# Third layer's loop on ScalarE: the output-weight product moved behind the squares, two convolution taps cut into halves and spread over four tiles

## The reference, cut to what matters

```python
proj = x @ W_in.T + b_in
gate, hBC, dt = proj[..., :INTER], proj[..., INTER:INTER+CONV_DIM], proj[..., INTER+CONV_DIM:]
hBC = silu(sum(xp[:, i:i+S, :] * conv_w[:, i] for i in range(K)))       # xp: hBC padded by K-1 in time
h, Bm, Cm = ...                                                         # split of hBC
...                                                                     # chunked recurrence over time -> y
g = y * silu(gate)
g = g * rsqrt(mean(g * g) + EPS) * norm_w
return g @ W_out.T + b_out
```

## Time and profile before

| | |
|---|---|
| median of 3 runs | 1243.27 us (1240.24 to 1246.04) |
| the profiled execution, its own time | 1239.47 us |
| its span, first to last instruction | 1237.7 us |
| mean granted clock of PE | 0.974 of full speed |
| busy | PE 90%, DVE 72%, ACT 65%, POOL 46% of the span |
| the loop of the third layer | from about 616 to 1060 us of the span, convolutions of tiles 3 to 31 start at 670.00 to 1044.48 |

### The profile page before, as it was taken

The page is one execution under the profiler, slowest core; times in us unless marked ns, Lnnn a source line. Parts: engine busy times, 40 slices in busy tenths (PEclk is TensorE's granted clock), DMA queues, the critical chain, the costliest instruction groups (busy, mean ns, idle before and its releaser), DMA issues.

```text
span 1237.7 us, 14557 instructions
## 1 busy us (share of the span) xinstructions
PE 1116.7 (90%) x4908; PEld 603.6 (49%) x4908; DVE 896.4 (72%) x1364; ACT 804.3 (65%) x1185; POOL 564.5 (46%) x310
## 2 busy tenths in 40 slices
PE   6778899999988999999788999999999999995887
PEld 1323344444334444444465666666666666432554
DVE  3657999999985444424677999899999999324454
ACT  4557667676644443323777999999999999436432
POOL 6002799898951955532014445545545545400000
PEclk8879899999999999999999999999999999998999
DMA  3000655555551211110021112112111111000000
GB/s 127 1 1 15 204 186 178 189 184 192 177 197 45 74 37 43 43 47 1 9 55 55 53 46 60 53 45 60 51 47 60 49 49 48 6 1 1 1 1 34
DMA packets 36664, 84.22 MB, mean 68 GB/s; under 512 B 7109, under 2 KB 13030, under 8 KB 36326
## 3 DMA queue, kind: packets, MB, share of 16 engines
q1 hardware_dynamic: 36590, 83.29, 21.1%
HBM read 80.72 MB, written 2.56 MB: 67 GB/s over the span
## 4 chain that ended last, share of the span: by engine, by line
PE 42%; DVE 28%; ACT 12%; POOL 8%; issue 8%; DMA 1%; SPq 0%; DVEq 0%; POOLq 0%; ACTq 0%
POOL work L729 6%; DVE work L1629 5%; PE ps L1002 4%; PE ps L1018 3%; PE ps L1010 3%; PE ps L1256 3%; DVE work L1701 3%; DVE work L1713 2%; DVE yd L1724 2%; DVE work L668 2%; DVE work L1727 2%; DVE work L1679 2%; PE ps L449 2%; PE ps L1965 2%; ACT work L1462 2%
## 5 line engine op out<-in xcount | busy, mean ns | idle before, releaser
L1800 POOL TENSOR_TENSOR ssum<-ssum,rs 128x1024 f32<-128x1024 f32 x32 | 75.9, 2371 | 205.1 <-DVE work L1629 202.8
L668 DVE TENSOR_TENSOR_SCAN work<-ps,work 128x1024 f32<-128x1024 f32 x64 | 146.6, 2290 | 8.3
L1629 DVE SCALAR_TENSOR_TENSOR work<-work,w_t 128x1024 f32<-128x1024 f32 x96 | 123.3, 1284 | 21.9 <-ACT work L1462 19.3
L449 PE MATMUL ps<-work,ident 128*128 128x512 f32 x256 | 121.7, 598 | 5.6 <-POOL work L729 5.6
L992 POOL TENSOR_TENSOR work<-work,ssum 128x1024 f32<-128x1024 f32 x32 | 76.3, 2389 | 105.6 <-DVE work L1081 57.9
L565 ACT ACTIVATE ps<-work,A 128x1024 f32<-128x1024 f32 x64 | 71.6, 1118 | 72.1 <-DVE work L668 72.1
L1081 DVE TENSOR_TENSOR work<-work,ps 128x512 f32<-128x512 f32 x64 | 43.8, 687 | 99.8 <-PE ps L1010 99.8
L1060 ACT ACTIVATE work<-ps 128x512 f32<-128x512 f32 x64 | 38.1, 597 | 115.4 <-PE ps L1002 115.3
L729 POOL TENSOR_TENSOR work<-work 128x1024 f32<-128x1024 f32 x42 | 99.1, 2362 | 13.6 <-DVE work L668 12.6
L1808 POOL TENSOR_TENSOR yd<-yd,work 128x896 f32<-128x896 f32 x32 | 67.0, 2092 | 45.9 <-DVE work L1727 45.9
L1713 DVE SCALAR_TENSOR_TENSOR work<-ps,work 128x512 f32<-128x512 f32 x128 | 81.9, 681 | 0.0
(11 more groups left out here) (358 smaller groups left out, 2541.5 us busy)
## 6 DMA issues: line engine op xcount, KB each, us to landing
work<-bc_rows SPq DMA_DIRECT2D x42, 512.0 KB, 3.6
work<-sdo_rows SPq DMA_DIRECT2D x64, 224.0 KB, 3.6
yd<-bc_rows SPq DMA_DIRECT2D x22, 512.0 KB, 3.6
rs<-w_rows SPq DMA_DIRECT2D x32, 256.0 KB, 4.1
ssum<-share_rows SPq DMA_DIRECT2D x32, 256.0 KB, 3.1
w_t<-in_tile_w SPq DMA_DIRECT2D x32, 195.5 KB, 2.6
work<-in_w SPq DMA_DIRECT2D x1, 2048.0 KB, 7.6
shared<-in_f SPq DMA_DIRECT2D x3, 512.0 KB, 6.1
```

The source lines that it names most:

```text
L449: mm = pe.matmul(ps[:, YACC + h, :], ident[:, :], HS[u % 4][:, h * BL:(h + 1) * BL], start=(n == 0), stop=(n == DS - 1))
L668: dve.tensor_tensor_scan(h, flat_pair(DABANK), h, 0.0, ALU.mult, ALU.add).then_inc(m0["scan"], 1)
L1629: c = dve.scalar_tensor_tensor(HC[u], HP[:, tap:tap + SEQ], par(u, "taps", tap), HC[u], ALU.mult, ALU.add)
L1800: pool.tensor_tensor(ssum[:, b, :], ssum[:, b, :], rs[:, :, :].rearrange("p k t -> p (k t)"), ALU.add).then_inc(m2["ss"], 1)
```

## The change

In ACT's step, `weights_out` moves from the end of step n, where it made the weights of tile n+1, to the middle of the step, behind `squares(n-1)`, where it makes those of tile n. The call ahead of the loop goes. `bc_first_tap` for the second sequence is cut into four calls of 512 positions, issued between `silu_gate` and `silu_h` in steps 1, 2, 4 and 5; before, two calls of 1024 positions stood at the ends of steps 2 and 3. DVE's wait for the taps follows.

```diff
+        B1_TAP = {1: (0, 0), 2: (0, 1), 4: (1, 0), 5: (1, 1)}
...
-            def bc_first_tap(b, m):
+            def bc_first_tap(b, m, half=None):
                 act.wait_ge(m2["bc_pad"], 4 * (b + 1))
-                source = pad[:, m, K3:K3 + SEQ] if b == 0 else src1[m]
-                act.activation(BCH[m][:, b * SEQ:(b + 1) * SEQ], source, ACT.Copy, scale=V("bc_conv", m * DC + K3)).then_inc(m2["bc_tap"], 1)
+                if half is None:
+                    to, source = BCH[m][:, 0:SEQ], pad[:, m, K3:K3 + SEQ]
+                else:
+                    to, source = blk(BCH[m], 2 * b + half), blk(src1[m], half)
+                act.activation(to, source, ACT.Copy, scale=V("bc_conv", m * DC + K3)).then_inc(m2["bc_tap"], 1)
...
                 if n >= 1:
                     squares(n - 1, 1 - u)
+                weights_out(n, u)
                 if more:
                     silu_gate(n + 1, 1 - u)
+                    if n in B1_TAP:
+                        bc_first_tap(1, *B1_TAP[n])
                     if n in B1_SILU:
                         bc_silu(1, *B1_SILU[n])
                     silu_h(n + 1, 1 - u)
...
-                    weights_out(n + 1, 1 - u)
-                if n in (B1_CONV - 1, B1_CONV):
-                    bc_first_tap(1, n - B1_CONV + 1)
...
             exponentials(0)
-            weights_out(0, 0)
...
-                    dve.wait_ge(m2["bc_tap"], 3 + m)
+                    dve.wait_ge(m2["bc_tap"], 4 + 2 * m)
```

## The result

The changed kernel has a median of 1234.22 us over 8 runs (1232.28 to 1239.06), beside 1244.17 us over 8 runs of the kernel before. The ratio is 0.9933, with a 95% interval of 0.9906 to 0.9959: 8.3 us less on 1243.27, with an interval of 5.1 to 11.7. Forecast were 1237.0 us and a gain of 6.3.

The account below looks back on a forecast made before the run. The circle convolution, transposes, shares, exponentials, `pad_h` was taken to set the pace in plain periods, with ACT delaying 19 of 32 convolutions. Gains 3.0 + 1.5 + 1.8 = 6.3 us off 1243.27 gave 1237.0 us, range 1232 to 1241.

Parts of the forecast that it names:

- part 3: `weights_out` leaves the path ahead of `pad_h` in 16 further steps; gain 1.8 us, bounds 0 and 4.8.
- Part 1: Steps 1 to 2: ACT's 3.3 us wait in `weights_out(2)` for `sum_out(0)` goes; gain 3.0 us, bounds 2.5 and 3.65.
- Part 2: Steps 2 and 3: first taps no longer delay `pad_h`, halves cost nothing; gain 1.5 us, bounds 1.4 and 2.4.
- Part 4: SP's next weights load goes out about 4 us later but lands 4.8 us early; cost 0.
- Rival A: PE sets the circle in plain periods, so the total gain is 4.0 us, 1239.3 us; chance 0.23.
- Rival B: All of `weights_out` comes back as `pad_h` starts sooner behind its product; gain 9.9 us, 1233.4 us; chance 0.17.
- Rival C: Weights land too late and PE waits in some 28 steps; slower, about 1265 us; chance 0.03.
- Rival D: The half taps on ACT are not covered and cost 4.0 us; gain 2.3 us, 1241.0 us; chance 0.12.

Follow-up runs that it names:

- e9: The changed kernel, unchanged, run again; median 1235.37 us of 12 runs, ratio 0.9939 to the kernel before.
- e3: The kernel before with only `weights_out(2)`, the call that waited 3.3 us, moved to the new place; 1238.26 us in one run.
- e2: The changed kernel with `weights_out` back at the end of the step, so only the taps are cut and moved; median 1240.53 us, ratio 0.9986.
- e1: The kernel before with `weights_out` moved, the first taps still whole at the ends of steps 2 and 3; median 1231.18 us, ratio 0.9927.
- e7: The changed kernel with the two first taps whole, between `silu_gate` and `silu_h` in steps 2 and 5; 1238.69 us in one run.
- e4: The changed kernel with `weights_out` making only one column of 128 from tile 2 on; 1234.8 us in one run.
- e5: The changed kernel with `weights_out` of tile n at the end of step n, so the next weights load starts later; 1403.0 us.
- e0: The kernel before, unchanged, run again for its trace; 1246.62 us.
- e8: The changed kernel with DVE's first convolution tap cut into halves for the 16 tiles that waited for ACT; median 1233.2 us, ratio 0.9916.

## Why the prediction was right, point by point

The measured median of 1234.22 us lies in the stated range of 1232 to 1241, but 1.3 us below the 1235.5 to 1238.5 that the forecast had for itself. Faster by over 0.5%, as it came out, had been given 0.43, and within 0.5% 0.52. The mechanism held; the sum was too low in one term (part 3), and the medians of whole executions add a difference of about 1 us that the loop does not explain.

Like with like, that is before and e9, both with the half clock on the shares of step 1, the loop gained 46.70 - 42.37 = 4.33 from tile 2 to 5 and 346.28 - 343.54 = 2.74 from 5 to 31: 7.1 us, with 6.3 forecast.

- **Part 1, the large wait: 3.0 forecast, 3.0 measured** in e3, where only this call is moved. The step by which PE takes back part of the 3.65 at the convolution is there too: 3.45 gained at tile 3, 0.44 given back at tile 4. After has it as well: its tile 4 takes 14.15, where the next one takes 13.43.
- **Part 2, the taps: 1.5 forecast, 1.3 measured** alone (e2), 0.6 on top of the product (e1 against e9), since the moved product by itself already takes 46.70 - 42.97 - 3.0 = 0.7 from the same two steps. Part 1 and 2 together were forecast at 4.5 and came to 4.3. The halves cost nothing that shows at their place, as said; that they had to be halves was not needed (e7).
- **Part 3, the sixteen steps: 1.8 forecast, 2.74 measured.** This is the mis-sized term. For tiles 10, 16, 17, 24 and 31 the step was right, 0.16 to 0.18 each, and tile 18 gave the forecast 0.29. Too low were three counts. Tiles 11 and 12 gained 0.18 and 0.23, where I had 0 for a `silu_h` that ends 0.1 late. It is late (in the plain period of after it starts at 769.26, straight behind the half Silu, with DVE done with the convolution before 769.05), and PE's transposes and DVE's second weighing with it, but `shares` needs only the first weighing and stands 6.86 behind the convolution as before; in e4 a product shorter by 0.11 changes nothing there. Tiles 27 to 29 gained 0.14, 0.23 and 0.16 with 0.08 each forecast, tile 30 0.19 with 0.04, tile 14 0.15 with 0. I had held `project_h` to a fixed distance behind `shares`, and only the bias copy was to move. Steps 25 and 26, PE of before, then PE and ACT of after:

```profile
984.95 1.80 PE L1256 MATMUL ps<-work 128*128 128x128 f32 x14
...
987.60 1.02 PE L1224 MATMUL ps<-work,w_t 128*128 128x512 f32 x2
```

```profile
983.80 1.80 PE L1257 MATMUL ps<-work 128*128 128x128 f32 x14
...
986.39 2.19 PE L1225 MATMUL ps<-work,w_t 128*128 128x512 f32 x4
...
987.46 0.69 ACT L1461 ACTIVATE work<-ps,w_t 128x512 f32<-128x512 f32 x1
```

  The bias stands 1.07 behind the projection, as predicted. But the projection is 986.39 - 983.80 = 2.59 behind `shares`, where it was 987.60 - 984.95 = 2.65 before, and one step on it is 2.51 against 2.65 again. With the 0.08 forecast for the bias that gives 0.14 and 0.22, and 0.14 and 0.23 were measured for tiles 27 and 28, so the missing part is the distance from `shares` to the projection. Between the two stand the last `arguments` (L1240 in before), and they shrink by as much: 0.73 us before (at 986.59), 0.68 and 0.60 after (at 985.44 and 998.76). ACT's copy comes 0.3 earlier and PE waits less for it, so PE's transposes and DVE's second weighing and masks come earlier as well, and these `arguments` wait less for the masks. That last reading is argued from the rows; no run isolates it.
- **Part 4, what is moved: 0, and 0 was measured.** The load goes out 3.9 us later in after (about 4 was said) and nobody waits for it; e5 shows what a wait there costs.
- **Rival A** (PE sets the circle, 4.0) fails for the plain steps, which went to 12.81. **Rival B** (9.9) fails for the same reason. **Rival C** is real as a mechanism, with its point where the load lands after PE wants the weights; after issues 7.7 us ahead of that, e5 1.1 us behind it. **Rival D** (halves not covered) fails by e2, where the taps alone gain 1.3 us.
- **The remaining difference to the measured 8.3** (7.6 in the second comparison) is within the intervals. A part can be the change's own by way of the clock: in e0 a half-clock stretch follows the stall that the change removes, and tile 4 comes 15.25 behind tile 3, against 14.11 in before. e0 came into the loop with more half clock than the first trace of before did (22.60 and not 19.65 between the convolutions of tiles 0 and 1), and so did after (22.61); after then shows no stretch in the steps up to tile 5, and neither do e7 and e8, which have no stall either and came in with 22.60 and 22.59. If that goes with the stall, the change is worth 46.64 - 41.19 = 5.45 there and 8.2 in all. Whether the stall brings the stretch, or both traces chanced on their patterns, stays open: of the kernels with the stall only one trace, e0, came in that way.

The signs named in the prediction were there: no wait in `weights_out`, the wait ahead of tile 3 at 1.42 (about 2 was said), a new wait on DVE for PE of 0.22 (0.4 was said), a shorter wait in `silu_h` (mostly 0.33 where it was mostly 0.62; 0.5 was said), tiles 4 and 5 without a wait, a total near 12 (11.5).

## What to carry to other kernels

Follow a small instruction that others do not need yet to what it stands in front of, and ask which engine it waits for: one product of 0.4 us held ScalarE for 3.3 us, and moving it in that one place out of 32 was worth 3 us. When it is taken out of a circle, the gain is not its own length but the distance to the next limit, here the 1.07 between a projection and its reader, and that gave 0.18 for 0.30; then check the other waits in the circle, which may shrink with it. Where a measurement scatters by 0.3% and the gain is 0.5%, compare distances between two instructions inside the traces; here they repeat to some 0.05 us in 350.

## What the runs showed of the hardware

The scatter around the median of after goes with PE's clock: the 8 runs of after ordered by time have mean granted clocks of 0.972, 0.971 and 0.973 at 1232.3 to 1232.6 us, 0.970 at 1234.2 and 1234.3, and 0.967, 0.965 and 0.967 at 1237.4 to 1239.1. Within the loop one half-clock stretch costs 1.2 us (42.37 against 41.19, same kernel). In these traces PE's last wait alone does not say whether one comes: PE waits 3.1 us ahead of the transposes of step 1 (L1249 in before) in before, e0 and after alike, and behind that the shares take 3.02 us in the first and 1.80 in the other two.

In e5 PE stood for 3.8 us in the mean in each period of 18 to 20 us, and its clock fell again and again, to a mean of 0.86 over 300 us. With waits of at most 0.8 us in the same stretch of after it was granted 1.00 throughout. The Trainium skill (TensorE: Matmul & The Clock Gate, Part 1: The HAM clock gate) describes a clock gate that lets fewer pulses through after PE has been little used; the traces agree (0.86 and 1.00). Here it made a late load dearer than its landing time alone: the mean period between tiles 5 and 31 grew from 343.5 / 26 = 13.2 to 489.3 / 26 = 18.8, by 5.6 us, of which the wait is 3.8 and the projection at half clock another 1.75 (3.65 and 1.90).
